# Routing weights by transfer, output bias by GpSimd: a two-layer decoder with three expert stages on one core

## The chip, the cores and the metric

The kernel runs on one core of a Trainium2 chip. The metric is the device time of one execution in microseconds (us); the median of three runs of the kernel before is 447.8 us.

## The reference, cut to what matters

Four sequences of 256 tokens with 256 features, x (4, 256, 256), go through two layers of three steps each. After every step stands a residual and a layer norm:

```
x = LN(x + linear attention(x), with output projection and o_b)      # layer 0
x = LN(x + four "experts" of context, chosen by token id)
x = LN(x + sum over 8 experts of gold weight * (silu(x Wg) * (x Wu)) Wd)     # called f0
x = LN(x + grouped attention(x))                                     # layer 1
x = LN(x + cross attention to the context)
x = LN(x + sum over 8 experts of combine weight * ... + shared expert)       # called f1
```

In f1 the hidden rows of the 8 experts (176 each) are one long list:

```
combine = zeros(T, 8) with the softmax scores of the two best experts of each token
act = silu(gu[..., :F]) * gu[..., F:]
y = einsum('tef,te,ehf->th', act, combine, down_weights)
y = y + silu(x sg) * (x su) @ shared_down.T
```

The change touches two things: how `combine` reaches the hidden rows of f1, and where `o_b` of layer 0 is added.

## The kernel before

All tensors are float32; for accuracy every product is made three times with the parts of a split: a rounded "high" part (type fp32r) and the "low" rest. ScalarE (ACT) makes high parts by a copy, GpSimd (POOL) makes low parts by a subtraction, TensorE (PE) multiplies high*high, high*low and low*high.

Each of the five instruction queues (SP for transfers, PE, ACT, POOL, DVE) works through an order written out by hand: the strings `SP_ORDER`, `PE_ORDER`, `ACT_ORDER`, `POOL_ORDER` and `DVE_ORDER` at lines 113 to 163. A step is a letter and a number. With s the number of a hidden chunk of 128 rows by 512 tokens (0 to 75; from 48 on they belong to f1): `g` and `u` are the gate and up products (six products of 512 columns each, lines 455 to 458), `d` the down product (24 or 12 of 256 columns, lines 718 to 720), `s` the silu on ACT (line 1038), `m` the product of silu and up on VectorE (DVE, line 1567), `h` and `l` the high part (ACT, line 1050) and low part (POOL, line 1253) of the hidden chunk, `a` the weighted add onto the tokens (DVE, line 1581). `G` and `D` load and split a weight pack (ACT lines 1068 and 1079, POOL lines 1259 and 1264, SP lines 375 to 396). Names with a dot are side work: `b` the first attention, `n` its norm, `r` the gold routing of f0 (`r0.5` and `r1.5` are `gold_weights`, some 30 small DVE instructions at lines 1603 to 1622), `a0.` and `a1.` the second attention, `e` the norms and the cross attention by example.

The tokens are worked on in two halves of 512. f1 has 14 chunks per half: three shared ones and 11 routed ones (22 routed over both halves). For a routed chunk the weights of the experts must lie over the chunk's 128 rows, for all 512 tokens. Before, this is a product: DVE makes `stack` (the weights in a high and a low part, lines 1786 to 1788), PE transposes it (line 898), ACT copies it to `cwT` (line 1163), and for each routed chunk PE multiplies `cwT` by a selector matrix that comes with the weight pack (line 673). DVE reads the result from a PSUM bank and multiplies the silu by it (`o` steps, `weighted`, line 1547). The four banks 0 to 3 are turned over by this: gate, weights and up of consecutive chunks take bank 3m, 3m+1 and 3m+2 modulo 4.

The bias `o_b` is added in the first attention by one more product per token tile, a matrix of ones with the bias row (line 595, 8 times), inside `a0_project` (steps b0.9 and b1.9). Its high and low rows are made at lines 992 and 1473.

Of the kernel before, what the change touches and what calls it, by code (L numbers as in the profile page):

```python
# [7 lines left out]
F32 = mybir.dt.float32  # L8
# [8 lines left out]
P = 128  # L17
# [35 lines left out]
G_F1, GLO_F1, D_F1 = 2 * D + P, 2 * D, D  # L53
# [60 lines left out]
S0 G0 D0 G1 D1 S1 G2 D2 G3 D3 G4 D4 G5 D5 G6 D6 G7 D7 G8 D8 G9 D9 G10 D10 G11 S2 D11 G12 S3 D12 G13 D13 G14 D14 R0 G15  # L114
R1 D15 G16 G17 G18 S4 G19 G20 G21 G22 G23 G24 G25 G26 R2 G27 R3 G28 G29 G30 G31 G32 G33 G34 G35 G36 G37 G38 G39 G40
G41 G42 G43 O0
""".split()
PE_ORDER = """
b0.0 b0.1 b0.2 b0.3 b0.4 b0.5 b0.6 b0.7 b1.0 b0.8 b1.1 b0.9 b1.2 b1.3 b1.4 b1.5 b1.6 b1.7 n0.2 b1.8 g0 g1 b1.9 g2 g3
d0 g4 n1.2 g5 g6 d1 g7 g8 d2 g9 g10 d3 g11 g12 d4 g13 d5 r0.2 g14 g15 r0.3 g16 u16 d6 g17 u17 d7 g18 u18 g19 d8 u19  # L120
g20 u20 g21 u21 g22 u22 g23 d9 u23 r1.2 d10 g24 u24 r1.3 g25 u25 g26 d11 u26 d12 g27 u27 g28 u28 g29 u29 d13 g30 u30
g31 u31 d14 d15 g32 u32 g33 u33 e0.12 e1.12 g34 u34 a0.3 g35 a0.4 u35 d16 a0.5 a0.6 g36 a0.7 d17 a0.8 u36 g37 u37 g38
u38 g39 u39 g40 a0.10 d18 a0.25 u40 g41 a0.11 u41 g42 a0.26 d19 d20 u42 g43 e0.2 e1.2 u43 e0.3 g44 e1.3 u44 g45 u45
e0.4 e1.4 d21 e0.5 e1.5 g46 u46 g47 u47 d22 e0.7 e1.7 d23 a0.22 g48 u48 g49 u49 e2.12 e3.12 g50 u50 a0.24 a1.3 a1.4
d24 d25 a1.5 a1.6 a1.7 g51 u51 a1.8 g52 u52 g53 u53 d26 d27 a1.10 d28 g54 a1.25 u54 g55 a1.11 u55 g56 a1.26 u56 g57
d29 u57 d30 e2.2 d31 e3.2 d32 e2.3 e3.3 g58 u58 g59 e2.4 e3.4 u59 e2.5 e3.5 g60 d33 d34 e2.7 e3.7 u60 g61 u61 a1.22
d35 d36 d37 g62 u62 g63 u63 a1.24 g64 u64 g65 d38 u65 g66 d39 d40 d41 u66 g67 u67 g68 u68 g69 u69 g70 d42 d43 d44 d45
# [28 lines left out]
a8 m19 r1.0 m20 m21 a9 m22 a10 r1.2 m23 r1.3 m24 r1.4 m25 a11 m26 a12 m27 m28 m29 r1.5 m30 a13 m31 a14 a15 e0.10 e1.10
m32 c e0.12 e1.12 a0.3 m33 a0.4 m34 a16 a0.5 m35 a0.6 a0.7 a17 m36 a0.8 m37 a0.9 m38 a18 a0.10 a0.25 m39 m40 a0.11 m41
a0.26 a19 e0.0 e1.0 a20 m42 e0.2 e1.2 m43 e0.3 e1.3 m44 m45 e0.4 e1.4 a21 e0.5 e1.5 m46 m47 a22 e0.7 e1.7 a23 e2.10
a0.22 e3.10 m48 a0.23 e2.12 e3.12 m49 a1.3 a1.4 m50 a1.5 a1.6 a1.7 o51 m51 a1.8 o52 m52 a1.9 o53 m53 a1.10 a1.25 o54
m54 o55 m55 e2.0 a1.11 a1.26 o56 m56 o57 e3.0 e2.2 e3.2 m57 e2.3 e3.3 o58 m58 e2.4 e3.4 e2.5 e3.5 o59 m59 o60 e2.7  # L160
e3.7 m60 o61 m61 a1.22 a1.23 x0 m62 m63 m64 o65 m65 y0 o66 m66 o67 m67 o68 m68 o69 m69 o70 m70 o71 m71 o72 m72 o73 m73
o74 m74 o75 m75 w0 w1 z1
# [3 lines left out]
def decoder_program(nc, x_rows, x_cols, ids, pad_mask, w_attn0, w_attn1, bias_cols, bias_rows, bias_v1,  # L166
                    w_route, temperature, consts, pk_x0, pk_f0, pk_x1, pk_f1, out):
    with ExitStack() as ctx:
# [3 lines left out]
        def sem(name):  # L172
# [37 lines left out]
        b_o = pr_lo[:, 0, :]  # L210
# [8 lines left out]
        brow = sb("brow", [P, 3 * D])  # L219
# [126 lines left out]
        def _(sp):  # L346
# [59 lines left out]

            out_v = out.rearrange("(t p) d -> p t d", p=P)
# [30 lines left out]
        def _(pe):  # L438
# [143 lines left out]
            def a0_project(h):  # L582
# [3 lines left out]
                for t in range(HT):  # L586
                    o = q_bank(h, t // 2)[:, (t % 2) * D:(t % 2 + 1) * D]
                    for kc in range(KC):
# [5 lines left out]
                        pe.matmul(o, al, wh, start=False, stop=False)  # L594
                    m = pe.matmul(o, ones_r, b_o, start=False, stop=True)
# [45 lines left out]
            def gate(s):  # L641
# [9 lines left out]
                if S_F0 + 2 <= s <= S_F1:  # L651
# [1276 lines left out]
```

## Time and profile before

| | |
|---|---|
| median of 3 runs | 447.8 us (446.67 to 448.8) |
| the profiled execution's own time | 447.0 us |
| its span in the profile | 445.2 us |
| PE busy | 425.5 us, 96% of the span |
| PE weight loads busy | 368.0 us, 83% |
| DVE, ACT, POOL busy | 256.1, 247.3, 265.5 us (58%, 56%, 60%) |
| mean granted clock of PE | 0.988 |
| transfers | 35.22 MB, 79 GB/s on average |

How to read it: busy time of an engine is the time in which one of its instructions runs; products are pipelined, so the distance from one start to the next says more about PE's speed than the duration of one. The row of the granted clock shows whether PE ran at full speed. A row of the timeline gives start, duration, engine, line, operation and tiles, and in brackets how long the engine had been idle and who released it.

### The profile page before, as it was taken

How to read it: one execution, taken by the hardware profiler on the slowest of the kernel's cores; microseconds unless marked ns; L12 is line 12 of the kernel's file. 1: busy time of each engine (PE TensorE's matmuls, PEld its weight loads, DVE VectorE, ACT ScalarE, POOL GpSimd, SP SyncE). 2: the span in 40 equal slices, each digit the busy share in tenths (PEclk: the TensorE clock that was granted, in tenths of full speed). 3: DMA queues.
4: the chain of work that ended last, by engine and by line, in shares of the span. 5: the costliest groups of instructions: out<-in, count | busy, mean ns of one | idle time of the engine just before them, and what ended most of it. 6: DMA issues, size and time to landing. Idle time of an engine off the chain costs nothing.

```text
span 445.2 us, 9339 instructions
## 1 busy us (share of the span) xinstructions
PE 425.5 (96%) x3668; PEld 368.0 (83%) x3668; DVE 256.1 (58%) x642; ACT 247.3 (56%) x423; POOL 265.5 (60%) x235
## 2 busy tenths in 40 slices
PE   7999999999999989899989999999999999999994
PEld 5788889988899878698869899697888889788884
DVE  5558656648555487666446578646454687242343
ACT  4656664665567534452734866841735945655443
POOL 2106379554767649673766479643685647667754
PEclk9999999999999989999989999999999999999998
DMA  8412403021232303331120215311041405141302
GB/s 256 123 49 79 135 1 106 14 71 50 71 96 71 119 24 119 118 99 45 49 87 16 65 43 155 98 41 46 10 133 54 124 1 153 56 121 52 118 1 94
DMA packets 15767, 35.22 MB, mean 79 GB/s; under 512 B 2123, under 2 KB 6091, under 8 KB 15724
## 3 DMA queue, kind: packets, MB, share of 16 engines
q1 hardware_dynamic: 15248, 34.00, 24.7%
q10 hardware_dynamic: 476, 0.63, 0.5%
q8 instruction: 29, 0.48, 0.4%
q14 instruction: 14, 0.11, 0.1%
HBM read 33.05 MB, written 1.05 MB: 77 GB/s over the span
## 4 chain that ended last, share of the span: by engine, by line
PE 70%; DVE 10%; ACT 6%; POOL 5%; DMA 4%; issue 3%; SPq 1%; ACTq 0%; DVEq 0%; POOLq 0%
PE bank L455 12%; PE bank L456 11%; PE bank L458 11%; PE bank L718 7%; PE bank L720 7%; PE bank L719 7%; DMA pk_raw<-w_attn_dram 1%; PE bank L782 1%; DVE stats L1383 1%; DVE hraw L1567 1%; DMA state<-o_tok 1%; PE bank L737 1%; PE bank L794 1%; DMA pk_raw<-pk_f_dram 1%; ACT L1038 1%
## 5 line engine op out<-in xcount | busy, mean ns | idle before, releaser
L1253 POOL TENSOR_TENSOR h_lo<-hraw,h_hi 128x512 fp32r<-128x512 f32 x76 | 97.8, 1292 | 66.5 <-ACT h_hi L1050 66.5
L455 PE MATMUL bank<-xT_hi,pk_hi 128*128 128x512 f32 x256 | 103.0, 402 | 1.4 <-DVE hraw L1567 1.1
L456 PE MATMUL bank<-xT_hi,pk_lo 128*128 128x512 f32 x256 | 101.7, 397 | 0.0
L1050 ACT ACTIVATE h_hi<-hraw 128x512 fp32r<-128x512 f32 x76 | 47.8, 629 | 77.4 <-DVE hraw L1567 72.1
L1259 POOL TENSOR_TENSOR pk_lo<-pk_raw,pk_hi 128x512 fp32r<-128x512 f32 (+1 forms) x44 | 74.6, 1696 | 15.6 <-ACT pk_hi L1068 15.6
L1567 DVE TENSOR_TENSOR hraw<-bank,sil 128x512 f32<-128x512 f32 x76 | 52.3, 688 | 52.4 <-ACT sil L1038 23.3
L458 PE MATMUL bank<-xT_lo,pk_hi 128*128 128x512 f32 x256 | 81.1, 398 | 0.0
L718 PE MATMUL bank<-pk_hi,h_hi 128*128 128x256 f32 x272 | 78.8, 290 | 2.2 <-DVE x_tok L1581 1.8
L720 PE MATMUL bank<-pk_hi,h_lo 128*128 128x256 f32 x272 | 77.6, 285 | 0.0
L719 PE MATMUL bank<-pk_lo,h_hi 128*128 128x256 f32 x272 | 77.6, 285 | 0.0
L455 PEld LDWEIGHTS bank<-xT_hi,pk_hi 128*128 128x128 f32 x256 | 48.5, 189 | 12.8 <-issue 1.7
L458 PEld LDWEIGHTS bank<-xT_lo,pk_hi 128*128 128x128 f32 x256 | 48.6, 190 | 11.6
L1038 ACT ACTIVATE sil<-bank 128x512 f32<-128x512 f32 x76 | 44.9, 590 | 23.5 <-PE bank L458 23.4
L1264 POOL TENSOR_TENSOR pk_lo<-pk_raw,pk_hi 128x256 fp32r<-128x256 f32 (+1 forms) x44 | 41.3, 939 | 27.5 <-ACT pk_hi L1079 27.5
L456 PEld LDWEIGHTS bank<-xT_hi,pk_lo 128*128 128x128 f32 x256 | 48.6, 190 | 9.9
L718 PEld LDWEIGHTS bank<-pk_hi,h_hi 128*128 128x128 f32 x272 | 52.6, 194 | 4.2 <-issue 2.4
L719 PEld LDWEIGHTS bank<-pk_lo,h_hi 128*128 128x128 f32 x272 | 52.8, 194 | 0.9
L720 PEld LDWEIGHTS bank<-pk_hi,h_lo 128*128 128x128 f32 x272 | 52.7, 194 | 0.0
L1068 ACT ACTIVATE pk_hi<-pk_raw 128x640 fp32r<-128x640 f32 (+1 forms) x44 | 37.4, 849 | 13.7 <-PE bank L458 11.2
L1079 ACT ACTIVATE pk_hi<-pk_raw 128x256 fp32r<-128x256 f32 (+1 forms) x44 | 21.7, 493 | 31.3 <-PE bank L720 30.8
L1581 DVE SCALAR_TENSOR_TENSOR x_tok<-bank,gold,x_tok 128x256 f32<-128x256 f32 x64 | 27.5, 478 | 19.1 <-PE bank L720 19.1
L1547 DVE TENSOR_TENSOR sil<-bank,sil 128x512 f32<-128x512 f32 x22 | 15.2, 690 | 34.4 <-PE bank L673 19.3
(263 smaller groups left out, 736.6 us busy)
## 6 DMA issues: line engine op xcount, KB each, us to landing
pk_raw<-pk_f_dram SPq DMA_DIRECT2D x28, 448.0 KB, 3.4
pk_raw<-pk_f_dram SPq DMA_DIRECT2D x16, 512.0 KB, 3.5
pk_raw<-pk_f_dram SPq DMA_DIRECT2D x16, 256.0 KB, 2.6
kv_buf<-pk_x_dram SPq DMA_DIRECT2D x4, 512.0 KB, 3.5
x_tok<-x_rows_dram SPq DMA_DIRECT2D x1, 1024.0 KB, 9.5
pk_raw<-pk_x_dram SPq DMA_DIRECT2D x4, 256.0 KB, 5.8
out_dram<-x_tok SPq DMA_DIRECT2D x4, 256.0 KB, 2.1
kv_buf<-w_attn_dram SPq DMA_DIRECT2D x1, 768.0 KB, 4.3
```

Source lines behind the costliest of these rows:

```text
L455: pe.matmul(o, w(kc)[0], x(kc)[0], start=kc == 0, stop=False)
L456: pe.matmul(o, w(kc)[1], x(kc)[0], start=False, stop=False)
L458: m = pe.matmul(o, w(kc)[0], x(kc)[1], start=False, stop=kc == KC - 1)
L718: pe.matmul(o, hh, vh, start=closed and kc == 0, stop=False, skip_group_check=not closed)
L719: pe.matmul(o, hh, vl, start=False, stop=False, skip_group_check=not closed)
L720: m_ = pe.matmul(o, hl, vh, start=False, stop=closed and kc == chunks - 1, skip_group_check=not closed)
L1038: A(sil[:, s % 2, :], src[:, :], ACT.Silu).then_inc(sems["silu_done"], 1)
L1050: A(h_hi[:, row, at * 512:(at + 1) * 512], hraw[:, s % 2, :], ACT.Copy).then_inc(sems["hid_hi"], 1)
L1253: pool.tensor_tensor(h_lo[:, row, q], hraw[:, s % 2, :], h_hi[:, row, q].bitcast(F32), ALU.subtract).then_inc(sems["hid_lo"], 1)
L1259: pool.tensor_tensor(g_part(kind, i, pk_lo)[:, 0:w], raw_g(kind, i)[0][:, 0:w], g_part(kind, i, pk_hi)[:, 0:w].bitcast(F32), ALU.subtract) ...
L1264: pool.tensor_tensor(d_part(kind, i, pk_lo), raw_d(kind, i)[0], d_part(kind, i, pk_hi).bitcast(F32), ALU.subtract).then_inc(sems["d_lo"], 1)
L1567: TT(hraw[:, r, :], other[:, :], sil[:, r, :], ALU.mult).then_inc(sems["hid_mul"], 1)
```

## The change

- f1's weights: `stack`, `cw_r`, the selector matrices in the weight pack and the 22 products at line 673 go. PE transposes the float32 weights themselves (8 rows), ACT copies them to `cwT`, SP saves them to device memory (`W0`, `W1`: 8 rows of 512), and for each routed chunk SP reads back the row of each expert in it, broadcast over the expert's rows of the chunk (`C` steps: 18 transfers per half, 256 KB per chunk), into one of two buffers `cw_all`. `weighted` multiplies the silu by that buffer. A chunk's `C` step waits until the chunk two before it has used the buffer.
- With the bank of the weights free, f1 uses banks like f0: gate in bank 0 or 2, up in bank 1 or 3, and f1's gate waits for the silu of two chunks before.
- Bias: the 8 products at line 595 and their preparation go. A row `bo1`, broadcast to 128 partitions by one more transfer, is added to `x_tok` by two POOL instructions (`p5`, `p6`) of 128x1024 each, before the attention's result is added.
- The five orders are written anew from end to end. Among the moves: `r1.5` from before m30 to after m32; `c` (constants: lines 1451 to 1456, without the memset of `cwT`) from before to after e0.12 and e1.12; b1.0 and b1.2 on PE earlier, b1.2 now ahead of b0.9; `X0` to `X3` on POOL ahead of `n0.0`; `S0` later.

```diff
+def experts_of(k):
+    n = (k % N1 - CH_S) * P
+    return [(e, max(n, e * F1) - n, min(n + P, (e + 1) * F1) - n) for e in range(n // F1, (n + P - 1) // F1 + 1)]
+def weights_landed(k):
+    r = routed_no(k)
+    return 16 * sum(len(experts_of(j)) for j in range(k + 1) if routed(j) and routed_no(j) % 2 == r % 2)
 SP_ORDER
-G41 G42 G43 O0
+R1 G16 ... G21 W0 C3 C4 S4 G22 C5 G23 G24 C6 G25 G26 R2 C7 C8 C9 R3 G27 C10 G28 G29 C11 C12 G30 C13
+G31 G32 G33 G34 W1 G35 C17 C18 G36 C19 C20 G37 G38 G39 C21 G40 C22 G41 C23 C24 G42 C25 G43 C26 C27 O0
 PE_ORDER
-... b1.7 n0.2 ... g31 u31 d14 d15 g32 u32 g33 u33 e0.12 e1.12 g34 u34 a0.3 g35 a0.4 u35 d16
+... b1.2 b0.9 b1.3 ... g31 u31 d14 d15 g32 u32 g33 u33 g34 e0.12 e1.12 u34 g35 u35 a0.3 d16
-... g62 u62 g63 u63 a1.24 g64 u64 g65 d38 u65 g66 d39 d40 d41
+... g62 d37 u62 g63 a1.24 u63 g64 u64 g65 u65 d38 g66 d39 d40 d41
 DVE_ORDER
-... a12 m27 m28 m29 r1.5 m30 a13 m31 a14 a15 e0.10 e1.10 m32 c e0.12 e1.12 a0.3 m33
+... m28 a13 m29 m30 m31 a14 a15 e0.10 e1.10 m32 r1.5 m33 e0.12 e1.12 m34 c a0.3
+            def save_weights(h):
+                sp.wait_ge(sems["cwT_done"], h + 1)
+                sp.dma_start(cw_dram[h, :, :], cwT[0:E1, :]).then_inc(sems["cw_saved"], 16)
+            def spread_weights(k):
+                h, r = k // N1, routed_no(k)
+                sp.wait_ge(sems["cw_saved"], 16 * (h + 1))
+                if r >= 2:
+                    sp.wait_ge(sems["m1_done"], r - 1)
+                for e, a, z in experts_of(k):
+                    sp.dma_start(cw_all[r % 2][a:z, :], cw_dram[h, e:e + 1, :].partition_broadcast(z - a)
+                                 ).then_inc(sems[f"cw_in{r % 2}"], 16)
-                    m = pe.matmul(o, ones_r, b_o, start=False, stop=True)
 def up(s)
-                    pe.matmul(bank[(3 * m + 1) % 4][:, :], g_part("f1", m, pk_hi)[:, 2 * D:2 * D + P],
-                              cwT[:, h * 512:(h + 1) * 512], start=True, stop=True).then_inc(sems["cw_ready"], 1)
+                pe.wait_ge(sems["hid_mul"], s - 1)
+                product(s, bank[2 * (s % 2) + 1][:, :], col, width, at).then_inc(sems["up_ready"], 1)
 POOL, prepare(5) and prepare(6)
+                    pool.wait_ge(sems["in_x"], 16)
+                    pool.wait_ge(sems["in_bo"], 16)
+                    pool.tensor_tensor(x_tok[:, q, :], x_tok[:, q, :], bo1[:, :].unsqueeze(1).to_broadcast([P, HT, D]),
+                                       ALU.add).then_inc(sems["x_biased"], 1)
 DVE, weighted(s)
-                dve.wait_ge(sems["cw_ready"], n)
-                TT(sil[:, r, :], bank[(3 * k + 1) % 4][:, :], sil[:, r, :], ALU.mult).then_inc(sems["m1_done"], 1)
+                dve.wait_ge(sems[f"cw_in{b}"], weights_landed(k))
+                TT(sil[:, r, :], cw_all[b][:, :], sil[:, r, :], ALU.mult).then_inc(sems["m1_done"], 1)
```

## Rows read from the trace of the kernel before

**Rows 1.** The page: busy time, share and instructions of each engine.
```profile
PE 425.5 (96%) x3668; PEld 368.0 (83%) x3668; DVE 256.1 (58%) x642; ACT 247.3 (56%) x423; POOL 265.5 (60%) x235
```

**Rows 2.** By stretch: PE, PEld, DVE, ACT, POOL busy; clock, DMA share, GB/s.
```profile
382.00:430.00 48.00, 48.00 (x259) 41.30 (x260) 17.28 (x32) 24.34 (x44) 34.92 (x32) 1.00 0.26 78
```

**Rows 3.** Timeline of PE in f1: start, duration, engine, line, operation.
```profile
404.51 0.40 PE L673 MATMUL bank<-cwT,pk_hi 128*128 128x512 f32 x1
404.75 0.39 PE L455 MATMUL bank<-xT_hi,pk_hi 128*128 128x512 f32 x1
...
407.53 0.28 PE L718 MATMUL bank<-pk_hi,h_hi 128*128 128x256 f32 x1
407.65 0.28 PE L719 MATMUL bank<-pk_lo,h_hi 128*128 128x256 f32 x1
```

**Rows 4.** Groups by line: count, busy us and mean ns, idle before.
```profile
L673 PE MATMUL bank<-cwT,pk_hi 128*128 128x512 f32 x22 | 9.2, 417 | 0.0
...
L595 PE MATMUL bank<-pr_lo 128*128 128x256 f32 x8 | 2.3, 284 | 0.0
...
L1547 DVE TENSOR_TENSOR sil<-bank,sil 128x512 f32<-128x512 f32 x22 | 15.2, 690 | 34.4 <-PE bank L673 19.3 <-ACT sil L1038 15.1
L1259 POOL TENSOR_TENSOR pk_lo<-pk_raw,pk_hi 128x1024 fp32r<-128x1024 f32 x16 | 38.4, 2402 | 3.8 <-ACT pk_hi L1068 3.8
```

**Rows 5.** Timeline: DVE's gold weights, PE's longest wait, and the clock after it.
```profile
153.81 0.17 DVE L1603 TENSOR_SCALAR zone<-inh 128x32 f32<-128x32 f32 x1
...
161.51 0.19 DVE L1622 TENSOR_TENSOR gold<-wz,s 128x32 f32<-128x32 f32 x1
...
160.91 0.63 PE L458 MATMUL bank<-xT_lo,pk_hi 128*128 128x512 f32 x2
163.36 0.36 PE L718 MATMUL bank<-pk_hi,h_hi 128*128 128x256 f32 x1 [1.82 <-DVE x_tok L1581]
...
164.00:168.00 4.00, 4.00 (x23) 4.00 (x22) 1.56 (x4) 0.66 (x2) 3.13 (x3) 0.57 0.00 0
```

**Rows 6.** Timeline: PE's wait behind DVE's constants.
```profile
179.34 1.35 DVE L1456 TENSOR_SCALAR bk_four<-con,bcol 128x4 f32<-128x4 f32 x1
...
180.21 0.62 PE L458 MATMUL bank<-xT_lo,pk_hi 128*128 128x512 f32 x2
182.18 0.47 PE L455 MATMUL bank<-xT_hi,wa_hi 128*128 128x512 f32 x1 [1.34 <-issue]
```

**Rows 7.** Timeline of the first stage: POOL, DVE, PE.
```profile
9.42 1.29 POOL L1229 TENSOR_TENSOR wa_lo<-pk_raw,wa_hi 128x512 fp32r<-128x512 f32 x1 [7.95 <-ACT wa_hi L972]
9.46 1.53 DVE L1473 TENSOR_TENSOR pr_lo<-brow,pr_lo 1x256 fp32r<-1x256 f32 x1
...
31.13 0.25 POOL L1245 TENSOR_TENSOR rw<-rw_raw,rw 128x32 fp32r<-128x32 f32 x1 [9.21 <-ACT rw L1004]
...
33.22 0.28 PE L595 MATMUL bank<-pr_lo 128*128 128x256 f32 x1
...
42.92 0.48 PE L455 MATMUL bank<-xT_hi,pk_hi 128*128 128x512 f32 x1
```

**Rows 8.** Timeline, second half: the weights' copy, and the first use.
```profile
381.20 0.59 ACT L1163 ACTIVATE cwT<-bank 16x512 fp32r<-16x512 f32 x1 [0.28 <-PE bank L898]
...
388.62 0.69 DVE L1547 TENSOR_TENSOR sil<-bank,sil 128x512 f32<-128x512 f32 x1 [2.80 <-PE bank L673]
```

**Rows 9.** The page: transfers, KB each, us from issue to landing.
```profile
pk_raw<-pk_f_dram SPq DMA_DIRECT2D x28, 448.0 KB, 3.4
...
pk_raw<-pk_f_dram SPq DMA_DIRECT2D x16, 256.0 KB, 2.6
...
x_tok<-x_rows_dram SPq DMA_DIRECT2D x1, 1024.0 KB, 9.5
...
out_dram<-x_tok SPq DMA_DIRECT2D x4, 256.0 KB, 2.1
...
bv<-bias_v_dram SPq DMA_DIRECT2D x1, 128.0 KB, 6.1
```

More of the change, by code:

```diff
@@ L117 @@
+G31 G32 G33 G34 W1 G35 C17 C18 G36 C19 C20 G37 G38 G39 C21 G40 C22 G41 C23 C24 G42 C25 G43 C26 C27 O0
 """.split()
 PE_ORDER = """
[L119 to L127, printed above, removed]
@@ L128 @@
-u70 g71 u71 g72 d46 u72 g73 u73 g74 u74 g75 u75 d47 e48 e49 e50 f48 e51 f49 f50 f51
+b0.0 b0.1 b0.2 b0.3 b1.0 b0.4 b0.5 b0.6 b0.7 b1.1 b0.8 b1.2 b0.9 b1.3 b1.4 b1.5 b1.6 b1.7 n0.2 b1.8 g0 g1 b1.9 g2 g3
+d0 g4 g5 n1.2 g6 d1 g7 g8 d2 g9 d3 g10 g11 d4 g12 g13 r0.2 g14 d5 r0.3 g15 g16 u16 d6 g17 u17 d7 g18 u18 g19 d8 u19
+g20 u20 g21 u21 g22 u22 d9 g23 u23 d10 g24 u24 g25 u25 r1.2 d11 r1.3 d12 g26 u26 g27 u27 g28 u28 g29 d13 u29 g30 u30
+g31 u31 d14 d15 g32 u32 g33 u33 g34 e0.12 e1.12 u34 g35 u35 a0.3 d16 a0.4 g36 u36 g37 a0.5 a0.6 u37 a0.7 g38 a0.8 d17
@@ new lines @@
+u38 g39 u39 d18 a0.10 g40 u40 a0.25 g41 u41 a0.11 d19 a0.26 g42 d20 u42 g43 u43 g44 e0.2 e1.2 u44 e0.3 e1.3 g45 u45
+g46 e0.4 e1.4 u46 e0.5 e1.5 d21 g47 u47 e0.7 e1.7 d22 a0.22 d23 g48 u48 g49 e2.12 e3.12 u49 g50 a0.24 a1.3 a1.4 u50
+d24 a1.5 a1.6 a1.7 g51 a1.8 u51 g52 u52 d25 d26 d27 a1.10 g53 u53 a1.25 g54 u54 a1.11 g55 u55 a1.26 d28 d29 d30 d31
+g56 u56 e2.2 e3.2 g57 e2.3 e3.3 u57 g58 u58 e2.4 e3.4 d32 d33 e2.5 e3.5 g59 u59 g60 u60 d34 e2.7 e3.7 g61 u61 a1.22
+d35 d36 g62 d37 u62 g63 a1.24 u63 g64 u64 g65 u65 d38 g66 d39 d40 d41 u66 g67 u67 g68 u68 d42 g69 u69 g70 u70 g71 d43
@@ L152 @@
+a1.8 l51 D20 G21 D21 G22 D22 G23 D23 l52 l53 e2.0 G24 l54 l55 D24 e3.0 e2.1 e3.1 G25 D25 G26 D26 l56 l57 l58 G27 D27
+G28 e2.5 e3.5 D28 G29 D29 l59 l60 G30 D30 G31 l61 D31 G32 D32 G33 l62 l63 D33 G34 l64 l65 D34 G35 D35 G36 D36 G37 l66
+D37 G38 D38 G39 l67 l68 l69 D39 G40 l70 D40 G41 l71 D41 G42 D42 G43 l72 l73 l74 D43 l75 y0 w0 w1
 """.split()
 DVE_ORDER = """
-p0 b0.0 b0.1 b0.2 b0.3 b0.4 b0.5 p2 b0.6 b0.7 b1.0 b0.8 b1.1 n0.0 b1.2 b1.3 b1.4 b1.5 b1.6 b1.7 n0.2 b1.8 p5 m0 m1
-n1.0 m2 a0 m3 m4 m5 n1.2 m6 a1 m7 m8 a2 m9 m10 a3 r0.0 m11 a4 m12 a5 m13 r0.2 m14 r0.3 r0.4 m15 a6 m16 m17 a7 r0.5 m18
@@ L156 @@
[L156 to L160, printed above, removed]
@@ L161 @@
-e3.7 m60 o61 m61 a1.22 a1.23 x0 m62 m63 m64 o65 m65 y0 o66 m66 o67 m67 o68 m68 o69 m69 o70 m70 o71 m71 o72 m72 o73 m73
-o74 m74 o75 m75 w0 w1 z1
+p0 p2 b0.0 b0.1 b0.2 b0.3 b0.4 b0.5 b1.0 b0.6 b0.7 b1.1 b0.8 p5 b1.2 n0.0 b1.3 b1.4 b1.5 b1.6 b1.7 n0.2 b1.8 m0 m1
+n1.0 m2 m3 a0 m4 m5 n1.2 m6 a1 m7 a2 m8 m9 a3 r0.0 m10 m11 a4 m12 r0.2 m13 a5 m14 r0.3 r0.4 m15 a6 m16 m17 a7 r0.5 m18
+a8 m19 m20 r1.0 m21 m22 a9 a10 m23 m24 m25 r1.2 a11 r1.3 a12 m26 r1.4 m27 m28 a13 m29 m30 m31 a14 a15 e0.10 e1.10 m32
@@ L1450, in later_constants @@
             def later_constants():
-                dve.memset(cwT[:, :].bitcast(F32), 0.0).then_inc(sems["cwT_zero"], 1)
                 link(dve.tensor_copy(cap[:, :, :], mask_w[:, :].bitcast(U8).rearrange("p (b s) -> p b s", b=B)))
```

167 lines of the change are left out of this document (73 added, 94 removed).

## Prediction, made before the changed kernel was run

> **What bounds the kernel now.** I read the page's busy times first: PE is busy for 425.5 of 445.2 us, no other engine above 60% [rows 1]. Then the busy time by stretch, because an average hides stages: in f1's second half PE is busy all 48 us at full clock, POOL 34.9, ACT 24.3, DVE 17.3 [rows 2]. Then PE's timeline, for the distance between starts, since durations overlap: a product of 512 columns takes 0.24 us until the next starts, one of 256 columns 0.12 us, though the rows say 0.40 and 0.28 [rows 3]. A gate or up product (six of 512) is thus 1.4 us, a down product of 12 parts 1.4 us. Last, PE's waits over 1 us in the timeline. The two largest in the middle of the kernel stand in [rows 5] and [rows 6]. So the kernel is bound by PE's work and a few waits; time taken off PE is time gained, except where a chain of other engines is the limit.
>
> **1. The selector products go.** 22 of them [rows 4], each 0.24 us apart from its successor [rows 3]: 22 x 0.235 = 5.2 us off PE, all in f1, where PE has no idle time [rows 2]. This is the sure part. The weight pack shrinks by 64 KB of 448, ACT's copy of it by 128 of 640 columns: off the path, counted at nothing.
>
> **2. The bias products go.** 8 [rows 4] x 0.12 = 1.0 us. Also the bias preparation on DVE: L1473, on one partition, took 1.53 us and holds up the first key product by some 0.5 us. Together 1.5 us, but the first stage ends in a chain: the last product before the first residual starts at 33.22, the first product on normed tokens at 42.92 [rows 7], 9.7 us of residual, statistics, POOL's root, ACT and transposes, with other products in between. The change puts b1.2 (1.4 us) ahead of b0.9, so this chain starts little earlier. I take 0.8 us. The two POOL additions of 128x1024 take 2.4 us each by the nearest group [rows 4]; POOL is idle for 9.2 us until 31.13 [rows 7], so 4.8 us find room before the residual. Price without that cover: up to 4.8 us. They wait for `x_tok`, issued early and landed after 9.5 us [rows 9], and behind them in POOL's queue are `p4`, `X0` to `X3` and `n0.0`; `X` (4 x 1.3) can be done before 36 us, when `n0.0` is wanted. Cost 0, bounds 0 and 2.
>
> **3. The routing weights by transfers.** What is removed on DVE (three small instructions per half, a memset) is about 1 us per half, hidden. What is added: 2 saves and 36 broadcast reads on SP's queue. For a landing the nearest rows are 2.6 us for 256 KB, 3.4 for 448 KB, 2.1 for a store; for a broadcast only the 6.1 us of the bias row, issued in the crowd of the start; the worst of all is 9.5 for 1 MB [rows 9]. I take 2.6 to 3.4, since nothing crowds the queues in f1 (DMA share 0.26, [rows 2]). The first use in the second half is the tightest: `cwT` is copied at 381.8 and used at 388.6, 6.8 us later [rows 8]. The new way needs save 2.2 + read 2.7 to 3.4 + issue and waking 0.5, so 5.4 to 6.1 us; in the new order four products (5.6 us) and a silu (0.6) lie between a1.24 and o65. If it comes late, DVE stands at o65 with m65 behind it, then ACT's h65, POOL's l65 and PE's d41; PE still has d38, g66, d39 and d40 first, some 2.8 us of slack beyond that. Cost 0, bounds 0 and 2. In the steady state two chunks take 48/11 x 2 = 8.5 us or so, and a buffer's loop is the landing + 0.9 us for `weighted` and waking = 3.5 to 4.3 us: hidden. SP is in order, and the `C` steps stand between loads of packs that wait for POOL's `D` steps; a `C` can be held by such a load (C23 behind G41, which waits for l69 and D39), by my walk 2 us late, under the 4.3 us of d43 to d45. R3 (the rolled output, which the next residual waits for) has C8 and C9 ahead: up to 1 us on a chain on which PE waits already. I count +0.5 us.
>
> **4. `weighted` reads two SBUF tensors** instead of PSUM and SBUF. Row: L1473, two SBUF inputs, 256 elements on one partition, started at 9.46 while POOL's L1229 ran from 9.42 to 10.71, and ended at 10.99 [rows 7]. It stood still until POOL was done. In f1 POOL is busy 73% of the time [rows 2] in pieces of 1.3 us, so a `weighted` waits 0.73 x 0.65 = 0.5 us on average and 1.3 at most. 22 x 0.5 = 10.3 us, if all lay on the path. It doesn't: DVE sat idle 34.4 us before these 22 instructions [rows 4], and the new order of banks gives PE more room (gate s waits only for silu s-2, up s for m s-2, four products or 5.6 us after gate s-2, against a chain silu 0.6 + weighted 0.7 + wait 1.3 + m 0.7 = 3.5 with waking). I take 0. The Trainium skill (SBUF — State Buffer, "Who interferes with whom") says the same of the cause: a VectorE instruction with two SBUF inputs and a GpSimd one that reads SBUF exclude each other. It speaks against this change, and by it the sum would rise by what rival A costs; the trace agrees, with the 1.53 us.
>
> **5. The new orders.** Before, `r1.5` ran from 153.8 to 161.7 on DVE, 7.9 us, with m30 and the adds behind it; PE's next product came at 163.36 where 161.4 was due (2.0 us), and then the granted clock was 0.57 of full speed over 164 to 168, half speed for most of it: 4 x 0.43 = 1.7 us more [rows 5]. 18 us later PE waited from 180.7 to 182.2 behind `c`, whose last instruction ended at 180.7, and the example lows behind that: 1.5 us [rows 6]. In the new order `r1.5` lies behind m32, and `c` behind the lows. From the end of u32, PE has g33 u33 g34, the transposes, u34 and g35 (7.6 us) before u35 wants m33, which comes after 0.7 + 5.8 to 7.9 + 0.7 = 7.2 to 9.3 us: a wait of 0 to 1.7 us, and then perhaps the low clock again. So of 5.2 us, between 5.2 and 1.8 are won there. The other moves are too many to walk through; each can open a wait of the kind that it closes elsewhere. I credit 2.0 us for all orders together, bounds 5.2 and -3.
>
> **Sum.** 447.0 (the profiled execution) - 5.2 - 0.8 + 0.5 - 2.0 = 439.5. The median stands 0.8 above that execution, so 440.3; I forecast 440.2.
>
> **Rivals.**
> A. *The exclusion of DVE and POOL lies on the path* (slower or equal). If each `weighted` delays the chain silu - m - h - l - d and PE meets it, the price is 22 x 0.5 = 10.3 us: 440.2 + 10.3 = 450.5, slower. It gives "slower" only from 9.8 us on (440.2 + 9.8 = 450.0), so nearly all 22 must hit; half of them give 445. For it: POOL is the second busiest engine in f1. Against: DVE's idle time before these instructions. 0.10 for 443 to 447, 0.05 for beyond 450.
> B. *Landings are long* (slower). If a broadcast from one row of device memory takes L, two chunks take at least L + 0.9 us against 8.5. Nothing happens up to L = 7.6; each us beyond costs 11 us. At 6.1, only the few pairs of gates with no or one down product between them lose some 1 us each, about 6 us: 446. At 9.5: 11 x 1.9 = 21, 461. It turns to slower at L = 8.5. Chance 0.04 for slower, 0.05 for about 446.
> C. *Only PE's work comes back*: the new orders lose as much as they win, or 2 to 3 us more. 447.8 - 5.2 - 0.8 + 0.5 = 442.3, to 445.5. 0.20.
> D. *The new orders close both waits and the clock's loss*: 440.2 - 3.2 = 437, with no new ones. 0.14.
> E. *No difference*: new waits of over 5 us anywhere, 446 to 449. 0.06.
> Forecast itself, 438.5 to 442: 0.36.
>
> **How the numbers follow.** Faster than 445.6 (0.5% below 447.8, about what a measurement can tell): forecast 0.36, D 0.14, C 0.20, the lower half of A's first case 0.07 and some of B's 0.03, so 0.80. Between 445.6 and 450.0: E 0.06, the rest of A and B 0.05, so 0.11. Above: A 0.05 and B 0.04, 0.09. Range: from 436, D's end with a margin for the unknown orders, to 446, where A's half and B's first case end.
>
> **What would show it.** Right: PE's matmuls down by 30; f1's second half shorter by 2.6 us at PE busy all through; no wait of PE after 160 over 2 us; `C` landings at 2.6 to 3.4 us. The exclusion: `weighted` with a mean over 0.69 us, up to 2.0. Wrong: PE rows in f1 released by DVE L1567 or by a `cw_all` transfer, or PE idle between 165 and 185 with a clock of 0.5 behind it; landings over 6 us.

## The result, and the profile after

The changed kernel takes 436.9 us (median of 4 runs, 434.4 to 438.3), the kernel before 448.05 beside it: ratio 0.975, 95% interval 0.972 to 0.979, so 11.2 us less. On another chip the same kernel gave 0.973 (0.969 to 0.976), 436.15 us. I had forecast 440.2, from 436 to 446.

| | before | after |
|---|---|---|
| profiled execution, own time | 447.0 us | 438.25 us (the longest of the four) |
| its span | 445.2 us | 436.3 us |
| PE's products | 3668 | 3638 |
| granted clock | 0.988 | 0.989 |
| transfers | 35.22 MB | 39.28 MB |

The page of the kernel after, busy time by engine (it answers [rows 1]), and the sums of its chain of waits by engine:

```profile
PE 417.6 (96%) x3638; PEld 363.4 (83%) x3638; DVE 260.0 (60%) x634; ACT 242.8 (56%) x422; POOL 275.3 (63%) x237
...
PE 82%; DVE 10%; issue 2%; ACT 2%; DMA 1%; POOL 1%; DVEq 0%; POOLq 0%; ACTq 0%
```

PE has 30 products fewer and 7.9 us less busy time, DVE and POOL more. PE is the bound as before.

Groups by line of the kernel after, shapes kept apart (count, busy us, mean ns, idle before): `weighted` from either buffer, to be held against L1547 in [rows 4], and POOL's two bias additions. Then the page's rows of the new reads:

```profile
L1560 DVE TENSOR_TENSOR sil<-cw_late,sil 128x512 f32<-128x512 f32 x11 | 13.4, 1216 | 17.2 <-ACT sil L1047 15.7 <-DMA cw_late<-cw_dram 1.5
...
L1560 DVE TENSOR_TENSOR sil<-brow,sil 128x512 f32<-128x512 f32 x11 | 10.5, 954 | 8.5 <-ACT sil L1047 8.5
...
L1253 POOL TENSOR_TENSOR x_tok<-x_tok,bo 128x1024 f32<-128x1024 f32 x2 | 4.8, 2404 | 1.3 <-DMA bo<-bias_o_dram 1.3
```
```profile
brow<-cw_dram SPq DMA_DIRECT2D x4, 256.0 KB, 3.7
...
cw_late<-cw_dram SPq DMA_DIRECT2D x2, 160.0 KB, 3.1
brow<-cw_dram SPq DMA_DIRECT2D x2, 160.0 KB, 3.6
```

The same 128x512 product took 0.69 us before and takes 0.95 and 1.22 on average now: 22 instructions cost 23.9 us of DVE instead of 15.2. One of them waited for a transfer, 1.5 us.

Where PE waited for over 0.8 us in the timeline of the kernel after, from 60 us on (start, duration, engine, line, operation, tiles; in brackets how long PE was idle and who released it):

```profile
177.19 0.50 PE L485 MATMUL bank<-xT_hi,pk_hi 128*128 128x512 f32 x1 [1.13 <-DVE hraw L1576]
...
185.36 0.50 PE L485 MATMUL bank<-xT_hi,wa_hi 128*128 128x512 f32 x1 [0.83 <-DVE q_buf L1654]
...
309.73 0.39 PE L488 MATMUL bank<-xT_lo,pk_hi 128*128 128x512 f32 x1 [0.96 <-issue]
...
315.38 0.30 PE L806 MATMUL bank<-kv_buf,pT 32*32 32x17 f32 x7 [2.73 <-issue]
...
426.90 0.36 PE L730 MATMUL bank<-pk_hi,h_hi 128*128 128x256 f32 x1 [1.03 <-POOL h_lo L1269]
```

(One more, 0.8 us near 280, is the second half's like of that at 185.) The waits of [rows 5] and [rows 6] are gone, and smaller ones stand at 177 and 185. Those at 309 and 315 are new and have no releaser; I call such a wait a stall. The first lies between the two last products of a gate (line 488), the second splits the 128 value products of one step. By stretch (PE, PEld, DVE, ACT, POOL busy; clock, DMA share, GB/s), the same four microseconds as in [rows 5], then the second of these stalls and what followed it:

```profile
164.00:168.00 4.00, 4.00 (x23) 3.42 (x22) 3.44 (x11) 1.23 (x2) 3.82 (x4) 1.00 0.63 189
```
```profile
311.40:315.40 4.00, 1.27 (x126) 1.13 (x125) 0.00 (x0) 0.00 (x0) 2.51 (x3) 0.87 0.81 247
315.40:321.00 5.60, 5.60 (x19) 3.97 (x18) 3.22 (x5) 1.75 (x3) 2.38 (x2) 0.50 0.20 59
```

After the stall PE ran 5.6 us at half speed (1.2 of 2.4 GHz), which costs it 2.8. The kernel before had such an event too, which I had not priced: within the value products of line 794, with this behind it (a row of the timeline, then one by stretch, both of the kernel before):

```profile
224.95 0.24 PE L794 MATMUL bank<-kv_buf,pT 32*32 32x17 f32 x5 [1.45 <-issue]
```
```profile
225.00:229.00 4.00, 4.00 (x16) 3.19 (x16) 1.97 (x4) 1.59 (x3) 3.05 (x2) 0.62 0.37 100
```

This profile of the kernel after has nothing at that place. But with the same order of PE's instructions e12, below, stood there 0.45 us and e7 1.66, both after 125 of the 128 products (timeline of PE, e7):

```profile
219.19 0.23 PE L806 MATMUL bank<-kv_buf,pT 32*32 32x17 f32 x3 [1.66 <-issue]
```

So where such a stall can lie is fixed by the program, and how long it is differs from one execution to the next. That the change removed the one in f0 is not shown. The one in f1's first half is the steady one: 1.9 to 2.7 us in all seven profiles of kernels with the new parts and orders and the new bias.

### The profile page after: what moved, and what is told of

Read it like the earlier page. It is cut to its first block, busy times and chain, and to the rows that moved or that the text cites. A ratio compares the mean times of both kernels' runs of the same rounds, so it can differ in the third digit from the quotient of the medians.

```text
span 436.3 us, 9331 instructions
## 1 busy us (share of the span) xinstructions
PE 417.6 (96%) x3638; PEld 363.4 (83%) x3638; DVE 260.0 (60%) x634; ACT 242.8 (56%) x422; POOL 275.3 (63%) x237
## 2 busy tenths in 40 slices
DMA packets 19335, 39.28 MB, mean 90 GB/s; under 512 B 2731, under 2 KB 6827, under 8 KB 19292
## 4 chain that ended last, share of the span: by engine, by line
PE 82%; DVE 10%; issue 2%; ACT 2%; DMA 1%; POOL 1%; DVEq 0%; POOLq 0%; ACTq 0%
PE bank L485 14%; PE bank L488 13%; PE bank L486 13%; PE bank L730 8%; PE bank L732 8%; PE bank L731 8%; PE bank L806 2%; PE bank L749 2%; DVE hraw L1576 1%; DVE sil L1560 1%; PE bank L794 1%; DMA q_buf<-x_cols_dram 1%; PE bank L508 1%; PE bank L780 1%; PE bank L779 1%
## 5 line engine op out<-in xcount | busy, mean ns | idle before, releaser
L1269 POOL TENSOR_TENSOR h_lo<-hraw,h_hi 128x512 fp32r<-128x512 f32 x76 | 99.8, 1316 | 79.6 <-ACT h_hi L1059 79.6
L730 PE MATMUL bank<-pk_hi,h_hi 128*128 128x256 f32 x272 | 77.8, 286 | 1.3 <-POOL h_lo L1269 1.0
L1280 POOL TENSOR_TENSOR pk_lo<-pk_raw,pk_hi 128x256 fp32r<-128x256 f32 (+1 forms) x44 | 43.6, 992 | 22.5 <-ACT pk_hi L1088 22.5
L1077 ACT ACTIVATE pk_hi<-pk_raw 128x512 fp32r<-128x512 f32 (+1 forms) x44 | 34.2, 778 | 8.8 <-DMA pk_raw<-pk_f_dram 5.6
L1229 POOL TENSOR_TENSOR rstd<-var_e,mhalf 128x2 f32<-128x2 f32 (+1 forms) x19 | 15.6, 820 | 21.5 <-DVE var_e L1392 12.7
```

Of the source, the lines that this page charges most:

```text
L730: pe.matmul(o, hh, vh, start=closed and kc == 0, stop=False, skip_group_check=not closed)
L1269: pool.tensor_tensor(h_lo[:, row, q], hraw[:, s % 2, :], h_hi[:, row, q].bitcast(F32), ALU.subtract).then_inc(sems["hid_lo"], 1)
L1280: pool.tensor_tensor(d_part(kind, i, pk_lo), raw_d(kind, i)[0], d_part(kind, i, pk_hi).bitcast(F32), ALU.subtract).then_inc(sems["d_lo"], 1)
```

## The experiments

All ratios are to the kernel before on the same chip. After's own are 0.975 and 0.973.

**Parts alone, orders alone.** The first keeps before's five orders and puts only the new steps in; the second has the old parts under the new orders.

```diff
e1: the kernel after, with the orders of the kernel before, and
+W0 C3 C4 G22 C5 G23 G24 C6 G25 G26 R2 C7 C8 C9 G27 R3 C10 ...   (SP)
+p1 p3 p5 p6 p4                                                    (POOL)
e2: the kernel before, with the orders of the kernel after without W, C, p5, p6
```

> All new parts (weights by transfer, bias by GpSimd, banks as in f0) with the five orders of before; only the steps W, C, p5 and p6 are put in. Theory 1 (the gain of 11 us is the removed products, about 6 us, plus about 5 us of waits that the new orders close before f1): this keeps the waits at 161 and 180 us with the low clock behind the first, and comes to 441 to 443 us. Theory 2 (the parts themselves give it all, the orders only fit them): 436 to 438 us. Theory 3 (the exclusion of DVE and POOL costs the removed products again unless the orders avoid it): 445 to 448 us.

> The kernel before with the new orders, without the steps that it has not (W, C, p5, p6): selector products, their bank rotation and the bias products stay. Theory 1: the waits at 161 and 180 us close, 442 to 444 us. Theory 2: the orders win nothing for the old parts, 447 to 450 us. With theory 1 the ratios of this one and of e1 multiply to about that of the full change, 0.975.

e1: 0.994 (0.991 to 0.997), 2.6 us gained. e2: 0.990 (0.982 to 0.997), 4.1 us. Together 6.7, so some 4.5 of the 11.2 us come only when both are there; by the three intervals that is 4.5 give or take 4, most of it from e2's. Against the prediction e1 is short: the parts alone should have given 5.5 us (442.3, rival C) and gave 2.6. That the exclusion of DVE and POOL ate the rest does not fit: `weighted` took 23.1 us in e1, less than the 23.9 in the kernel after. In both profiles I looked for what ate the rest. In e1 a read stood behind a load and a roll on SP's queue (timeline of DVE), and PE waited 3.63 us before line 509 at 341.72, where the kernel before waits 0.79. In e2 it is `c` (timeline of DVE, then of PE, then by stretch):

```profile
327.99 0.69 DVE L1561 TENSOR_TENSOR sil<-brow,sil 128x512 f32<-128x512 f32 x1 [5.06 <-DMA brow<-cw_dram]
```
```profile
181.90 2.77 DVE L1454 TENSOR_SCALAR cap<-cap 128x1024 f32<-128x1024 f32 x1
184.71 2.19 DVE L1455 TENSOR_SCALAR bk_four<-con,bcol 128x4 f32<-128x4 f32 x1
...
188.26 0.80 PE L454 MATMUL bank<-xT_hi,wa_hi 128*128 128x512 f32 x1 [3.85 <-DVE q_buf L1644]
```
```profile
188.00:193.00 5.00, 4.74 (x11) 3.81 (x12) 3.54 (x8) 0.00 (x0) 1.33 (x2) 0.50 0.45 151
```

The wait of 1.8 us at 161 is in e1 and not in e2. In the kernel after, without the memset in `c`, `cap` (L1470) started at 181.01, ahead of POOL's `xp_lo` at 181.30, and took 0.69 us; e2's started at 181.90, behind the same POOL instruction (181.73, 2.39 us), and took 2.77. e2 still has the memset, 0.91 us; the rest of the difference is one of phase. Together: 3.85 us of wait against 0.83, and a clock at half speed behind it. e2 also has a stall in f1's first half, 2.02 us at 315.98.

**Was e1's loss only my placing of a read?** In e1, C7 was issued at 324.0, behind G25, G26 and R2.

```diff
-... C6 G25 G26 R2 C7 C8 C9
+... C6 C7 G25 G26 R2 C8 C9
```

> e1_new_parts_old_orders again with one step of SyncE's order mended: C7 ahead of G25, G26 and R2, C9 still behind. In e1 C7 was issued only at 324, behind the loads and behind R2, which waits for the attention's output, and a `weighted` stood 5.1 us for it. Theory (the new parts give little under the old orders because a read behind a load or a roll makes its own wait): that wait goes, 2 to 4 us come back: 441.5 to 443.5 where e1 gave 445.6. Rival (the old orders of PE, VectorE and ScalarE, not the place of the read, hold the parts' gain back): within 1 us of e1, 444.5 to 446.5.

0.992 (0.989 to 0.996), 444.85 us. The DMA wait went (the same `weighted` started at 323.5), but the time fell by 0.7 us only; PE's wait before line 509 near 340 shrank from 3.6 to 2.1 us, and the two of before are there, at 162 and 180 (1.82 and 1.33 us). The rival holds: it is not the place of this read. Which of the old orders keep the parts' gain back was not taken apart further.

**The two moves in the kernel before.** To make room, m33 moves ahead of the lows too.

```diff
-... m29 r1.5 m30 a13 m31 a14 a15 e0.10 e1.10 m32 c e0.12 e1.12 a0.3 m33
+... m29 m30 a13 m31 a14 a15 e0.10 e1.10 m32 r1.5 m33 e0.12 e1.12 c a0.3
```

> The kernel before with only three of DVE's steps moved: the gold weights r1.5 to behind m32 and m33 behind them, the constants c behind the lows e0.12 and e1.12. Theory 1 with these two waits as its cause (2.0 + 1.5 us and 1.7 us of low clock, less a new wait at m33): 443 to 446 us, PE's wait before the down product d14 gone and the clock at full speed over 164 to 168. Rival (many small moves give it): 447 to 449 us.

1.012 (1.006 to 1.018), slower by 5 us. At its new place `r1.5` lies beside POOL's long instructions and takes 11.4 us, from 172.0 to 183.4, where it took 7.9 before. That is 3.5 of PE's 8.67 us; the larger part is that in the old order of PE only g34 and u34 stand behind u33 before it needs the lows, which DVE now makes behind `r1.5` (timeline of DVE; then PE):

```profile
172.88 2.02 DVE L1608 TENSOR_SCALAR none_in<-s 128x4 f32<-128x4 f32 x1
...
176.84 1.20 DVE L1422 TENSOR_TENSOR zone<-con,top_f 128x32 f32<-128x32 f32 x1
177.97 2.38 DVE L1423 TENSOR_TENSOR pick<-con,top_f 128x32 f32<-128x32 f32 x1
...
185.62 0.77 PE L455 MATMUL bank<-xT_hi,wa_hi 128*128 128x512 f32 x1 [8.67 <-issue]
```

**The two moves taken back in the kernel after.**

```diff
-... m28 a13 m29 m30 m31 a14 a15 e0.10 e1.10 m32 r1.5 m33 e0.12 e1.12 m34 c a0.3
+... m28 a13 m29 r1.5 m30 m31 a14 a15 e0.10 e1.10 m32 m33 c e0.12 e1.12 m34 a0.3
```

> The kernel after with two steps of VectorE's order put back where they stood before: r1.5 before m30, and c before e0.12 and e1.12. All else as after. Theory (these two moves are worth what the waits of before cost, 1.8 to 5.2 us): wait of 1.8 us near 161 with the half clock behind it, and c ahead of the lows again: 439 to 442. Rival (the moves do nothing of themselves; the fit of the orders to the new parts does it): 436 to 438.

0.987 (0.984 to 0.989), 440.8 us: 1.1 to 1.4% or 5 to 6 us more than the kernel after, as the theory had it. (The profiled execution was the fastest of its six, 437.95: it has no half clock behind its stall.) PE's one wait in 155 to 190, and the stretch behind it:

```profile
165.20 0.55 PE L730 MATMUL bank<-pk_hi,h_hi 128*128 128x256 f32 x1 [5.60 <-POOL h_lo L1269]
```
```profile
165.00:170.00 5.00, 4.80 (x25) 4.83 (x26) 0.88 (x2) 0.22 (x1) 5.00 (x4) 0.57 0.27 79
```

So under the new orders `r1.5` ahead of m30 costs 5.6 us of wait and 2 of clock; where it stands it costs 1.1. The same two moves are worth 5 us among the new parts and orders and cost 5 among the old ones.

**The bias alone, and the bias back.** e4 is the kernel before with the bias by POOL; e10 the kernel after with the bias by products.

```diff
e4 (in the kernel before), e10 the reverse (in the kernel after)
-                    m = pe.matmul(o, ones_r, b_o, start=False, stop=True)
+POOL: p5 p6, x_tok += bo1
```

> The kernel before with the bias added by GpSimd alone (two additions of 128x1024, one more transfer into a corner of the buffer of the second attention's output, which is free at that time), all orders else as before. My step 2: 0.8 to 1.5 us less, 446.5 to 447.3. Rival (the chain of the first norm sets the end of the stage, or the additions are late): 448 or slower, with the first product on normed tokens no earlier than 42.9 us.

> The kernel after with the output bias back as it was before: 8 products, its preparation by ScalarE and VectorE, no additions by GpSimd; new orders and weights by transfers as in the kernel after. Theory (step 2 of the prediction: 0.8 us, 1.0 of products and 0.5 of a VectorE instruction held by GpSimd, part of it hidden): 0.5 to 1.6 us slower than the kernel after, with the first product on normed tokens that much later. Rival (under the new orders the bias change is worth nothing, as it was alone in e4): same as the kernel after within 0.4 us. Rival (it is the larger part of what is unexplained, 3 us): 439 to 440.

e4: 1.000 (0.996 to 1.003). The first product on normed tokens came at 41.34, 1.6 us earlier than before, and the lead stood at 1.7 to 1.9 until 270; then a stall like those above, at 319.36 in the value products (2.15 us, no releaser), took it. e10: 0.978 (0.975 to 0.980), against 0.973 (0.969 to 0.976) for the kernel after on the same chip: 1.4 to 2.1 us slower, though the two intervals overlap. First product on normed tokens, kernel after again (e12) and e10, timeline of PE:

```profile
40.23 0.48 PE L485 MATMUL bank<-xT_hi,pk_hi 128*128 128x512 f32 x1
```
```profile
41.86 0.48 PE L484 MATMUL bank<-xT_hi,pk_hi 128*128 128x512 f32 x1
```

1.6 us both ways. This start scatters, though. With the new orders it came at 40.05 to 40.76 in six profiles with the new bias and at 42.31 in one, at 41.68 and 41.86 in two with the old; with the old orders at 41.34 and 41.42 in two with the new bias and 43.16 in one, at 42.92 and 43.23 in two with the old. So the bias change is worth some 1.5 us in the first stage, twice my 0.8, and the time shows it only if nothing later takes it back.

**The exclusion of DVE and POOL.**

```diff
-                A(sil[:, s % 2, :], bank[2 * (s % 2)][:, :], ACT.Silu)
+                to = bank[2 * (s % 2)][:, :] if u_routed(s) else sil[:, s % 2, :]
+                A(to, bank[2 * (s % 2)][:, :], ACT.Silu)
-                TT(sil[:, r, :], cw_all[b][:, :], sil[:, r, :], ALU.mult)
+                TT(sil[:, r, :], bank[2 * (s % 2)][:, :], cw_all[b][:, :], ALU.mult)
```

> The kernel after, but for f1's routed chunks ACT writes the silu back into its PSUM bank, so that `weighted` reads one PSUM and one SBUF tensor, as before; in exchange the gate that uses the bank next waits for the `weighted` of two chunks before, in place of its silu. Theory (the stretching of `weighted` by POOL is hidden, except at the end, where one of 1.41 us pushed the last chunk): mean of `weighted` back from 0.95 to 1.22 us to 0.69, and 0.7 to 1.5 us off the whole: 435.4 to 436.2 where the kernel after gives 436.9. Rival (the exclusion costs on PE's path in many places): 22 x 0.4 = 8.7 us of VectorE time, of which half would come back: 432 to 433. Rival (all of it is hidden, the end too): 436.9.

0.970 (0.967 to 0.973), 433.9 us: 0.3 to 0.5% less than the kernel after, some 1.3 to 2.4 us. By itself that is hardly clear of noise, but e11, below, which keeps the edit, gives 0.969: the pair against the two measurements of the kernel after is 0.5% less, give or take 0.3. The group of `weighted`, and no wait of PE before the last product:

```profile
L1568 DVE TENSOR_TENSOR sil<-bank,cw_late 128x512 f32<-128x512 f32 x11 | 7.6, 692 | 19.2 <-ACT bank L1054 17.5 <-DMA cw_late<-cw_dram 1.7
...
L1568 DVE TENSOR_TENSOR sil<-bank,brow 128x512 f32<-128x512 f32 x11 | 7.6, 688 | 9.4 <-ACT bank L1054 9.4
```

In the kernel after, the last three `weighted` took 1.84, 1.40 and 1.41 us, each chain behind them a bit later, until PE waited 1.03 us for the last `h_lo`. With one input in PSUM all 22 take 0.69, and that wait is gone. From the second half's first routing product (line 749) to the last product, the six profiles of after, e6, e7, e8, e10 and e12 take 67.2 to 67.3 us, e5 and e11 66.1. From the first product on normed tokens to the last product, after took 387.4 us in both profiles, this one 386.1: 1.3 us, where 8.7 us of DVE's busy time came back. The rest had been hidden.

**The transfers, and the stall without a releaser.** e6 leaves out 14 of 18 reads per half; e7 moves two loads away from the stall.

```diff
e6, spread_weights
+                if k % N1 > CH_S + 1:
+                    return
e7, SP_ORDER
-C6 G25 G26 R2 C7
+C6 R2 G25 G26 C7
```

> The kernel after with the reads of the routing weights for the first two routed chunks of each half alone; the other chunks use what stands in the buffers, so that part of the weights is wrong: it leaves out 14 of the 18 transfers per half. Theory (reads cost nothing in the steady state; the stall of 2.7 us of PE at 312 within the value products is not of their making): 436.0 to 437.2, since the only wait of `weighted` for a transfer, 1.5 us, may go too. Rival (the reads crowd the stretch 309 to 316, in which PE's own instructions are fetched): the issue wait of 2.7 us at 312 and the half clock of 6 us behind it go, 2.7 + 3 = 5.7 us: 431 to 433.

> The kernel after with the loads G25 and G26 (2 x 384 KB) moved behind R2 in SyncE's order, so that they start at 317 or so and not at 311. Theory (PE's issue wait within the value products comes from the crowded transfers of 310 to 315, share 0.84): PE's 128 value products of line 806 at 311.5 run through, no half clock over 315 to 321, 3 to 5.5 us gained at 321, unless the packs, now 6 us later, come late: 432 to 434. Rival (the wait has nothing to do with the transfers, or recurs wherever a block of 128 small products is fetched): issue wait of 1.4 to 2.8 us still there, 436.9 or a little more.

e6: 0.971 (0.968 to 0.974), 434.5 us, 0.5 to 2 us less than the kernel after; the intervals overlap, so a cost of the reads of up to 2 us isn't excluded, the rival's 4 to 6 us is. e7: 0.976 (0.974 to 0.979), no change; its move made one `weighted` wait 4.5 us for C7, so the time alone says little here, but the stall is still there. It is in every kernel with the new parts and orders, whatever the transfers do, and three with the old parts or the old orders have one near there too: e4 2.15 us, e2 2.02, e1 0.49. By stretch, e7 around its stall and behind it, then the same of e8:

```profile
312.40:315.70 3.30, 1.39 (x129) 1.26 (x128) 0.00 (x0) 0.00 (x0) 2.42 (x3) 1.00 0.22 80
...
315.70:319.50 3.80, 3.80 (x17) 2.98 (x11) 2.31 (x5) 1.49 (x3) 0.78 (x1) 0.55 0.15 37
```
```profile
313.70:317.00 3.30, 1.38 (x129) 1.24 (x128) 0.00 (x0) 0.00 (x0) 2.38 (x3) 1.00 0.81 244
...
317.00:321.00 4.00, 4.00 (x117) 3.13 (x115) 2.48 (x5) 1.63 (x3) 0.94 (x1) 1.00 0.29 92
```

At a DMA share of 0.22 and of 0.81 PE stands 1.9 us after 121 of the 128 products; in e5 and e11 it is 1.9 too, in e6 and e12 2.2, in the profile of after 2.7. So crowded transfers do not make it. In the profile of after the stalls at 309 and 315 lie 128 products apart, 256 instructions with the weight loads. And in e10, with 8 products more ahead, the stall in this step comes after 113 products in place of 121 and is 0.64 us long, and the one before it comes in the value products of the step before, after 126 of 128 (timeline of PE):

```profile
310.23 0.23 PE L806 MATMUL bank<-kv_buf,pT 32*32 32x17 f32 x2 [2.31 <-issue]
```

The two together are 2.6 to 3.7 us in all eight profiles of kernels of this kind, e10 included. The table of DMA queues has one transfer of the instruction queue (q8, 16 KB) just ahead of the stall, and none within it. In the profile of after it runs between 312.4 and 312.5, and PE stands from 312.65 to 315.38. Its row for 311.3 to 312.8 (for 312.8 to 315.3 there is none):

```profile
q8 instruction: 1, 0.02, 6.1%
```

The same holds everywhere: over the 14 profiles, each of the 38 stalls of over 0.3 us behind 190 us has such a transfer ahead of it, and PE goes on 2.3 to 3.2 us after that transfer began, whether it had come to stand 0.1 or 2.4 us behind it. In f0 of the profile of after it began at 217.2, PE was through 125 products only at 219.6, and there is no stall. That PE stands until its own instructions are there fits all of this. No run here removes the stalls or moves such a transfer by itself, so it is argued, if strongly, and not shown. The half clock came behind the stall in after, e5, e6, e7, e11 and e12, not in e8 and e10.

**One more move on top.** e5 with `c` behind `a0.3`.

```diff
-... m34 c a0.3 a16 a0.4
+... m34 a0.3 c a16 a0.4
```

> e5_silu_in_bank with one more move: VectorE's step c, whose last instruction of 128x4 took 2.25 us beside GpSimd, stands behind a0.3 instead of ahead of it, so that the queries of the second attention (line 1662 there) come 4 us earlier and PE's wait of 1.0 us at 182 goes. Theory (the wait is really c's): 0.8 to 1.2 us less than e5. Rival (the next link of the chain, the keys behind c, is late in its place): the wait reappears within 5 us, no gain or a loss of up to 1.5 us.

0.969 (0.966 to 0.973), the same as e5. The wait of 0.83 us went, and a new one stood seven microseconds on (timeline of PE): the keys, now behind `c`.

```profile
191.16 0.39 PE L784 MATMUL bank<-wa_hi,xT_hi 128*128 128x256 f32 x1 [1.24 <-DVE kx L1672]
```

**After once more**, as the measure:

> The kernel after, unchanged, timed and profiled once more on the same chip as e9 to e11, as the measure for them. In its first profile the first product on normed tokens started at 42.3, in four kernels whose first stage is the same at 40.1 to 40.8: if that is the start's scatter, it starts at 40 to 41 here. PE's wait within the value products near 312 should be there again, 1.9 to 2.7 us, with or without the half clock behind it. Time 435.5 to 437.5.

436.15 us, profiled at 436.11. Its first stage was 2.1 us shorter than in after's first profile (40.23 against 42.31), as in e5 to e8 (40.05 to 40.76): so that much is scatter of the start. In after's first profile the products from 6.8 to 10 us start 0.43 us apart, in place of 0.23.

## Why the prediction came out as it did

With e12's profile, which lies at its median, the difference of PE's last product to the kernel before (427.58 against 438.63, 11.1 us) can be laid out by place. The sizes are gaps between starts in PE's timeline beyond the spacings of [rows 3], rounded; the row of f0's value steps is from the first's start to the fourth's, 15.80 against 13.41 us.

| place | us | forecast |
|---|---|---|
| to the first product on normed tokens | -2.7 | -0.8 |
| the four bias products behind it | -0.5 | in the -0.8 |
| waits and clock, 155 to 190 | -3.2 | part of -2.0 |
| other gaps before f0's value steps | -0.9 | |
| f0's value steps, with the stall and half clock of before | -2.4 | not seen |
| selectors | -5.2 | -5.2 |
| from f0's value steps to the second half's routing, with the new stalls and half clock, less before's waits | +3.8 | not seen |
| waits in the second half | 0 | 0 |
| sum | -11.1 | -7.5 with the +0.5 for transfers |

**Step 1, selectors: right, as far as it can be seen.** From the second half's first routing product to the last product took 69.8 us before (368.82 to 438.63) and 67.3 after (362.47 to 429.73), 2.6 us less, which is 11 x 0.235. The match is cleaner than it should be: a wait of 0.86 us of the kernel before (at 381.96) went as well, and the wait of 1.03 us at the end came. In e5, without that end, the stretch is 3.7 us shorter than before. In the first half the same 2.6 us were won and then buried under the new stalls.

**Step 2, bias: the term was too small.** Some 1.5 us by e4 and e10. I had argued that b1.2 ahead of b0.9 would keep the chain from starting earlier; with the old order as with the new it started some 1.5 us earlier. The rest of the 2.7 is the first stage's new order (e2: 1.2 us earlier). The additions took 4.77 us, from 14.55 on, behind a row that landed after 9.4 us; nobody waited.

**Step 3, transfers: right in sum.** 256 KB landed in 3.6 to 3.7 us, not 2.6 to 3.4. The tight place was the one named, the second half's first use: the copy of `cwT` ended at 373.95, and it was used at 379.84, 5.9 us on, inside my 5.4 to 6.1; DVE waited 1.5 us for it, and PE had work. In the kernel after no read behind a load hurt; under the old orders one did (5.1 us), by the mechanism that the prediction had for C23.

**Step 4, exclusion: the mechanism, its size and its cover were right, its end was missed.** 0.4 us per `weighted` (forecast 0.5), nearly all hidden, as counted. What I had not walked is the tail, where no down products stand between the last chain and PE: 1.2 us, shown by e5. The rule of the Trainium skill (SBUF — State Buffer, "Who interferes with whom") speaks of a VectorE instruction with two SBUF inputs; here the runs agree, with 0.69 us in e5 against up to 1.84. Instructions with a single tensor input were held too, as `bk_four` (128x4, 2.25 us) and `none_in` (128x4, 1.27 to 2.02 us); the same section allows that for `tensor_scalar`.

**Step 5, the orders: the term that was mis-sized.** All orders together gave 4.1 us among the old parts (e2) and 8 to 9 among the new ones (the kernel after against e1), beyond even my bound of 5.2. I credited 2.0 us, because each move can open a wait of the kind that it closes. e8 shows the two moves to be worth 5 us where they stand, since under the other new orders `r1.5` in its old place would cost 5.6, not 1.8. The new wait that I forecast at m33, 0 to 1.7, came with 1.13, and no low clock behind it. And e3 shows why the caution was not foolish: the same moves without the others lose 5.

So the forecast's missing 3.3 us are steps 2 and 5. That it missed by so little is partly luck: taken one after the other, parts and then orders, they gave 2.6 and 8 to 9 us where I had 5.5 and 2.0. What the sum had no place for is that the two depend on each other. Rival D (437) is the case that came nearest, and by its mechanism, both waits closed and the clock kept at 165 to 168; but its number too was met with luck. What neither it nor the forecast had are the stalls: 2.4 us less in f0, part of it the luck of the execution, and more than that, 3.8 with what else changed there, lost in f1.

Of the signs that I had named, the 30 products fewer, the 2.6 us of the second half and the mean of `weighted` came. "No wait of PE after 160 over 2 us" failed by the stall of 2.73 us, and full landings were 3.6 to 3.7 us, above my 3.4.

## What to carry to other kernels

A move in a hand-written order has no price of its own: the same two steps were worth +5 us or -5 us, by what the other engines ran beside them. Price the work that is removed, and measure an order only together with the parts that it was made for. When a cost is called hidden, walk the end of the kernel by itself, since there nothing covers it. And before a gain is credited, look for PE idle with no releaser and the clock behind it: such an event moves when the instructions ahead of it change in number, and its length changes from one execution to the next, so a single profile before and one after can't price it.

## What the runs showed of the hardware

- PE stood 1.9 to 2.7 us in the middle of 128 small products (32x17, 121 of which had run in 1.2 us), behind one 16 KB transfer of the instruction queue, at a DMA share of 0.22 as at 0.81; it went on 2.3 to 3.2 us after the transfer began, in all 38 such stalls of the 14 profiles. The Trainium skill (Runtime: NRT & Kernel Launch, "Instruction fetch mechanics") says that instructions are refilled in 16 KiB blocks of 256 and that this is mostly hidden. The size agrees: the queue made 29 such transfers in the kernel after, for 3638 products with a weight load each. If these stalls are such refills, they are not hidden here, where so many short instructions follow each other.
- The clock fell to half speed for 3 to 6 us behind idle times of PE of 1.3 to 5.6 us (1.27 in e4, 5.60 in e8), but not behind each: 1.00 after the 1.92 us in e8 and the 2.31 in e10, 0.55 after the 1.91 us in e7.
- A DVE instruction of 128x4 beside POOL took up to 2.25 us.
- One row of device memory read into 128 partitions, 256 KB, landed in 3.6 to 3.7 us in the middle of the kernel; the bias row, issued in the crowd of the start, in 9.4.
